# Two attention layers on a graph: the sums over edges as column-tile products, a quad's four units in a row behind the turns

## The reference, cut to what matters

```python
N, D, E = 3125, 64, 100000           # nodes, features, edges; edges are sorted by dst
def gatv2_layer(x, src, dst, Wl, Wr, att, bias, n_nodes, heads):
    xl = (x @ Wl).reshape(N, heads, Dh)
    xr = (x @ Wr).reshape(N, heads, Dh)
    e = leaky_relu(xl[src] + xr[dst], 0.2)
    logits = einsum('ehd,hd->eh', e, att)
    a = exp(logits - segment_max(logits, dst)[dst])
    alpha = a / segment_sum(a, dst)[dst]
    out = segment_sum(alpha[:, :, None] * xl[src], dst)
    return out.mean(axis=1) + bias
h = relu(gatv2_layer(x, ..., heads=8));  h = gatv2_layer(h, ..., heads=4)   # with self loops
x = layernorm(x + h)
# then: agg = segment_sum(x[src], dst); three dense layers; layernorm(x + that)
```

## Time and profile before

| | us |
|---|---|
| median of 3 runs | 4096.24 (4094.41 to 4099.37) |
| the profiled execution | 4089.57 |
| its span | 4087.8 |
| edge pass of layer 0, first fetch in it to the last of L831 | 188 to 1849 |
| edge pass of layer 1, the same | 2082 to 3501 |
| mean granted TensorE clock | 0.898 of full speed |

### The profile page before, as it was taken

One profiled execution on the slowest core, in us unless ns is written; L12 is line 12 of the kernel. 1 busy time (PEld: TensorE's weight loads), 2 busy tenths in 40 slices (PEclk: granted clock), 3 DMA queues, 4 the chain that ended last, 5 costly groups with the idle time before them and its releaser, 6 DMA issues. The chain is left out here.

```text
span 4087.8 us, 76312 instructions
## 1 busy us (share of the span) xinstructions
PE 3300.5 (81%) x24219; PEld 2212.1 (54%) x24219; DVE 2805.8 (69%) x6824; ACT 1702.7 (42%) x3682; POOL 2877.9 (70%) x2229
## 2 busy tenths in 40 slices
PE   0499999999999999995259877777777778557886
PEld 0246666666666666674236555554555555346663
DVE  3558888888888888876628755555555566478872
ACT  3254444444444444422124433333333332156651
POOL 4488888887777777423778888888888883568860
PEclk9899999999999999977579988888888887589897
DMA  2233333333333333322124433333333332112220
GB/s 58 50 65 87 81 88 86 87 86 85 88 85 84 82 87 85 71 63 74 43 50 87 83 70 72 68 68 68 67 69 72 68 69 44 36 34 44 43 48 28
DMA packets 612701, 277.99 MB, mean 68 GB/s; under 512 B 450601, under 2 KB 572877, under 8 KB 611716
## 3 DMA queue, kind: packets, MB, share of 16 engines
q1 hardware_dynamic: 263920, 103.06, 11.5%
q0 software_dynamic: 110784, 80.17, 11.2%
q10 hardware_dynamic: 237600, 89.88, 9.0%
HBM read 164.01 MB, written 106.40 MB: 66 GB/s over the span
## 5 line engine op out<-in xcount | busy, mean ns | idle before, releaser
L900 PE MATMUL L_e_ps_z<-L_e_xT,L_w_abs 128*128 128x500 f32 x2700 | 1499.9, 642 | 0.0
L825 POOL DMA_INDIRECT L_e_xs<-in_x_dram,src_idx x880 | 1192.0, 1355 | 339.3 <-issue 261.0
L825 POOL DMA_INDIRECT L_e_xs<-x_d,src_idx x820 | 1077.5, 1314 | 253.3 <-issue 249.7
L951 PEld LDWEIGHTS L_e_ps_v<-L_e_xs,L_e_p 125*128 125x128 f32 x5400 | 856.4, 203 | 628.2 <-issue 571.9
L995 ACT ACTIVATE L_e_rl<-L_e_ps_z 128x500 f32<-128x500 f32 x1350 | 793.0, 587 | 880.8 <-PE L_e_ps_z L900 880.8
L951 PE MATMUL L_e_ps_v<-L_e_xs,L_e_p 125*128 125x65 f32 x5400 | 792.9, 273 | 12.1 <-DVE L_e_acc L1179 10.6
L1179 DVE SCALAR_TENSOR_TENSOR L_e_acc<-L_e_acc,L_e_row,L_e_ps_v 128x130 f32<-128x130 f32 (+1 forms) x1440 | 450.1, 313 | 423.3 <-PE L_e_ps_v L951 282.0
L887 PE MATMUL L_e_ps_x<-ident,L_e_xs 125*64 125x125 f32 x1800 | 289.0, 286 | 309.6 <-DMA L_e_xs<-x_d,src_idx 253.1
L988 ACT ACTIVATE L_e_xT<-L_e_ps_x 128x500 f32<-128x500 f32 x450 | 264.3, 587 | 620.2 <-PE L_e_ps_x L890 603.3
L900 PEld LDWEIGHTS L_e_ps_z<-L_e_xT,L_w_abs 128*128 128x128 f32 x2700 | 426.5, 197 | 78.1 <-issue 24.5
L1162 DVE TENSOR_TENSOR L_e_p<-L_e_ohc,L_e_ae 125x640 f32<-125x640 f32 x540 | 427.4, 819 | 0.2 <-PE L_e_ps_v L951 0.2
(11 more groups left out here) (304 smaller groups left out, 3654.2 us busy)
## 6 DMA issues: line engine op xcount, KB each, us to landing
L_v_d<-L_e_acc ACTq DMA_DIRECT2D x225, 260.0 KB, 3.0
L_e_dlb<-dloc_d SPq DMA_DIRECT2D x90, 468.8 KB
L_v_d<-L_e_acc ACTq DMA_DIRECT2D x225, 130.0 KB, 2.8
L_e_xw<-x_d SPq DMA_DIRECT2D x1800, 12.0 KB
L_e_xs<-in_x_dram,src_idx POOLq DMA_INDIRECT x900
L_e_xs<-x_d,src_idx POOLq DMA_INDIRECT x900
L_e_lim<-limits_d SPq DMA_DIRECT2D x180, 39.1 KB
g_xs<-x_d,src_idx POOLq DMA_INDIRECT x240, 3.0
```

The costliest lines, as they stand in the source:

```text
L825: pool.indirect_dma_start(xs[c.slot(XR)][:, n, 0:D], None, lay.x_rows, bass.IndirectOffsetOnAxis(k.src_idx[:, u:u + 1], 0)).then_inc(gath[ ...
L900: pe.matmul(ps_z[part % ZR][:, 0:QT], lay.w_abs[:, part * 128:(part + 1) * 128], xT[q][:], start=True, stop=True).then_inc(s["z_ready"], 1)
L951: ins = pe.matmul(ps_v[u // 2 % 2][:, u % 2 * VX + v * XW:u % 2 * VX + (v + 1) * XW], p[st % 3][:, u % NQ, v, :, :].rearrange("e n h -> e ...
```

## The change

Each product of L951, with 128 weight columns, becomes two of 64: nodes 0 to 15 of the window into partitions 0 to 63 of `ps_v`, nodes 16 to 31 into partitions 64 to 127 (two column tiles of the array). The moving operand is the same 65 columns, now streamed for each half. The four units of a quad come one behind the other right behind `turn`, whose L890 writes to partitions 64 to 127 of its tile. The parts of `project` follow together, then the transposes for ACT, and `reduce` is last. Waits and counts of the semaphores are as they were, and so is the order on DVE, ACT, POOL and SP.

```diff
                     for v in range(HV):
-                        ins = pe.matmul(ps_v[u // 2 % 2][:, u % 2 * VX + v * XW:u % 2 * VX + (v + 1) * XW],
-                                        p[st % 3][:, u % NQ, v, :, :].rearrange("e n h -> e (n h)"),
-                                        xs[c.slot(XR)][:, u, :], start=True, stop=True)
+                        for half in range(2):
+                            ins = pe.matmul(ps_v[u // 2 % 2][64 * half:64 * half + 64, u % 2 * VX + v * XW:u % 2 * VX + (v + 1) * XW],
+                                            p[st % 3][:, u % NQ, v, half * WN // 2:(half + 1) * WN // 2, :].rearrange("e n h -> e (n h)"),
+                                            xs[c.slot(XR)][:, u, :], start=True, stop=True)
                     if n % 2:
                         ins.then_inc(s["v_ready"], 2)
...
-                    for part in range(4):
-                        if part % (4 // C) == 0 and (c.after(1) or q >= 1) and zc.there():
-                            project(zc, zq, part // (4 // C))
-                        if c.after(3) and bc.there():
-                            sums(bc, bq, part)
-                    if (c.after(1) or q >= 3) and rc.there():
-                        reduce(rc, rq)
+                    if c.after(3) and bc.there():
+                        for n in range(Q):
+                            sums(bc, bq, n)
+                    if (c.after(1) or q >= 1) and zc.there():
+                        for part in range(C):
+                            project(zc, zq, part)
...
+                    if (c.after(1) or q >= 3) and rc.there():
+                        reduce(rc, rq)
```

## The result

| | before | after |
|---|---|---|
| median of the runs, us | 4095.32 (4 runs, 4093.75 to 4099.37) | 4055.65 (4 runs, 4054.83 to 4067.52) |
| profiled execution, us | 4089.57 | 4054.83 |
| its span, us | 4087.8 | 4053.0 |

The ratio is 0.9907 with an interval of 0.9893 to 0.9922: 40 us less, clear of no change, half of the 79 us that the forecast gave, and just outside its range, which ended at 4055. The experiments ran on four chips, called the second to the fifth here (which chip the runs of this table used isn't known, so it may be one of the four).

The account below looks back on a forecast made before the run. TensorE was taken to bind layer 0 and the fetches layer 1, with fetches binding both after the change. 71 us (layer 0's last turn) + 5 + 3 (tails) = 79 less, 4096.2 - 79 = 4017, range 3978 to 4055.

Parts of the forecast that it names:

- What bounds the kernel: Layer 0: TensorE binds at 35.4 us a chunk, POOL's fetches 1.9 to 3.0 behind; layer 1: the fetches already bind.
- Two column tiles overlap: Edge sums in layer 0: loads and passes of both tiles run beside each other, 32 passes in 0.96 us.
- the two rivals of no overlap: Edge sums: tiles don't overlap, 1.85 us a body, 4155 (8%); loads don't overlap passes at all, 3.55 us, 4540 (2%).
- TensorE at 32.3 us a chunk: Layer 0: a body saves 0.62 us, a chunk of five 3.1, from 35.4 us.
- The fetches at 1.675 us: Layer 0: POOL's fetches bind at 33.5 us a chunk of 20; last chunk's turn at 1666 instead of 1737, 71 us less.
- The 5 us: Layer 0: allowance added to the slower fetch pace for a few more long fetches beside a denser VectorE.
- The closing sentence of the prediction: Sign of error: fetches longer by more than 0.05 us each once VectorE is denser, 44 us over 880.
- Layer 1's pace unchanged: Layer 1: fetches bind before and after, so the pace stays at 32.0 us a chunk.
- The tails: Work behind each layer's last fetches: 5 us less (0 to 8) in layer 0, 3 us (0 to 5) in layer 1.
- Handoff rival: Layer 0: handoff to VectorE or ACT eats part of TensorE's gain; 34.2 us a chunk gives 4043, range 4032 to 4088; 20%.
- Slower than before: Whole kernel: chance of a slower time, 0.10, from the rivals without overlap at 4155 (8%) and 4540 (2%).

## Why the prediction was right and wrong, step by step

- **What bounds the kernel: right.** TensorE was the bound of layer 0 and the fetches stood close behind. With the change the fetches are the bound: TensorE waits for them (43.8 us in 1100), and POOL's wait for the sums is gone.
- **Two column tiles overlap: right.** The 32 passes of a body start within 1.11 us (999.47 to 1000.58), for a forecast of 0.96 in all, and the two rivals of no overlap (4155, 4540) fall. The Trainium skill, TensorE: Matmul & The Clock Gate, under Part 3, has a load run beside matmuls in flight only where the row group differs. Here 32 loads and 32 passes in two column tiles that share all rows take 1.26 us by the body shown, where one behind the other was put at 3.55, so the trace disagrees.
- **TensorE at 32.3 us a chunk: 0.6 low.** Without the fetches it is 32.9, a gain of 2.5 and not 3.1: TensorE is busy for 31.9 and waits 1.0 for VectorE's `run`, a wait that the sum had at nothing. It didn't matter, as the fetches bind.
- **The fetches at 1.675 us: the step that failed.** The sum took the pace over from the kernel before and allowed 5 us for a few more long ones. The fetches came every 1.7025 us over the pass: the mean one took 1398 ns, where it was 1371 (548.32 us by 400) in the stretch that gave 1.675, and 1355 over the whole pass. The 5 us had to be 28, as the last fetch started at 1686 in place of 1663. The turn follows at 1690, for a forecast of 1666: 24 us of the gain missing. The reason given for the 5 us, a denser VectorE, was at most a small part of it: what counts is where the fetches begin against the scans, 44.0 us over the pass, and the others got shorter by 5.6. The closing sentence of the prediction, wrong if fetches get longer by more than 0.05 us each, names what came about, at 0.043 in layer 0.
- **Layer 1's pace unchanged: wrong by 15 us.** Its fetches went from 1.6191 to 1.6372 us each over 820, though its waits are for the same things as before; its forward scans now begin just ahead of a fetch (34 of 42 by under 0.5 us, where it was 9).
- **The tails: 5 and 3 forecast.** From turn to store 3.6 us were saved; behind layer 1's last turn nothing (677.2 us to the end of the span before, 677.9 after).
- **Sum:** 24 (turn) + 15 (layer 1's pace) + 1 and 4 us (the two tails) are missing from 79 in the profiled execution, which leaves 35; it measured 34.8. The medians differ by 40.
- **Handoff rival** (20%, 34.2 us a chunk, 4032 to 4088): its pace and time came out, and by another mechanism, so that is chance. PE waits for L1181 only 11.6 us in 1100 there; the handoff shows with the fetches gone.
- **Slower than before** (10%) was forecast for a layout that doesn't overlap. It came on one chip by late signals, which nothing in the trace of the kernel before points to.

## What to carry to other kernels

When a change moves the bound to the second engine in line, that engine's pace in the kernel before is no safe term: here it lost 38 us in layer 0 by beginning its fetches at other moments of the same VectorE instructions. Look for its long instructions, and at which moment of whose instruction they begin, and put a range on that. A gain of 1% should be timed on more than one chip.

## What the hardware showed that was not expected

- A fetch (indirect DMA issued by GpSimd) that begins within a VectorE scan over two SBUF operands ends 1.016 us after it (up to 2.4 us for 1.21); those that began more than 0.05 us ahead of the scan take 1.24 us in the mean. L1072, with one bf16 operand, holds fetches too; a reciprocal of one f32 operand mostly doesn't (22 of 27).
- Late signals of TensorE, 2.3 us by the median and up to 4.4, at the same place in 40 of layer 0's 45 chunks, on some chips and on others not at all: 4264 against 4056 us for the same kernel, with a mean granted clock of 0.882 and 0.877. The cause stayed open.
- The clock: the changed kernel's TensorE was granted the lower level (1.2 GHz) for 3.4 us ten times between 500 and 1600, about every third chunk, each time within a microsecond of a chunk's first turn that had waited 3.2 to 3.5 us for the fetches. After the 11 turns that had waited 0.8 to 1.0 us it wasn't, and before the change there was no such stretch there. The 32 passes of the sums from 1008.94 on start within 2.0 us in place of 1.1. The second line is the time up to the next such stretch:

```profile
1008.90:1012.30 3.40, 3.40 (x39) 2.76 (x39) 1.67 (x5) 0.59 (x1) 2.57 (x3) 0.50 0.22 37
1012.40:1111.20 98.80, 93.58 (x966) 52.63 (x964) 86.89 (x185) 50.83 (x107) 81.40 (x58) 1.00 0.41 91
```
